# The last task of a two-layer spectral kernel: rows loaded in three narrow transfers, held groups through three pairs of banks, three groups added by GpSimd

## The chip, the cores and the metric

The kernel runs on one core of one Trainium2 chip. The time is device microseconds of one execution; three runs of the kernel before took 517.57 us in the median (516.96 to 521.88). All arithmetic is float32.

## The reference

Input x is (4, 45, 90, 384): batch, height H = 45, width W = 90, channels. Two spectral layers follow each other, and the second starts from the first one's spectrum. In each, a 2-D real FFT over H and W goes to 23 kept columns of W, eight channel blocks of 48 pass through two small matrices with ReLU and softshrink, and an inverse FFT is added to the layer's input:

```python
xf = rfft2(x, axes=(1, 2), norm='ortho')              # 23 columns of W
o1 = relu(blocks(xf) @ w1 + b1)
z  = softshrink(o1 @ w2 + b2, 0.01)                   # second layer: complex
y  = irfft2(z, s=(H, W), axes=(1, 2), norm='ortho') + x
```

## The kernel before, in words

The work is cut into 8 tasks: 4 images times 2 halves of 192 channels. A task's image half lies in one of three SBUF tiles `img` as 90 partitions (w) by 45 x 192.

1. **fwd**: 12 groups of four rows of H (the last has one) are multiplied by the forward matrix of W, and go by way of `fs` (task 0: `f0`) to the scratch `scr_f` in HBM.
2. **Steps**: 23 columns of W make 6 steps of 4 columns a task, 48 steps in all, numbered s = 0 to 47. A step loads its columns into `bt`, and runs the products a, c0, d0, c1, d1, t and e (FFT over H, both layers' matrices, transposes, inverse FFT over H). The result of e is copied by ACT and DVE from bank pair P0 to `et`, and stored by SP to the scratch `scr_i` (L341). Task 7 is steps 42 to 47.
3. **rows** and **inv**: when the six steps of a task are stored, its 46 (48 with padding) rows, a real and an imaginary one for each column, are loaded back (L364) in 5 sets of groups of H, each set as two transfers of 48 partitions (even and odd pairs of rows of H, at partitions 0 and 64), into the three tiles `jr`. For each of 12 groups TensorE multiplies by the inverse matrix of W (L657; two matmuls, each seen as two records), and DVE adds the result to `img` (L587). Then y is stored: by GpSimd's queue for tasks 0 to 6, two groups at a time (L416), by SP's queue group by group for task 7 (L368).

`schedule()` writes one order of kinds by hand, and each engine and each DMA queue walks it in that order, doing its own part; semaphores hold it back. In the steady state the groups of inv of an earlier task stand between the products of a step. At the end no step is left to stand between:

- Task 6's groups g0 to g6 stand in steps 46, 47 and the drain; g7 to g11 ("held") come after e of step 47. All use bank pair P3 (banks 6 and 7), and L639 to L641 make TensorE wait for the add of the group before.
- Then `rows` of task 7: SP waits for the stores of steps 46 and 47 (L347), for each set also until the bank `jr` is free (L356, after a held group's product), for sets 3 and 4 in `bt` until the last a.
- Task 7's groups rotate through four bank pairs (P0 to P3). Groups 1, 4, 7 and 10 (`LAST_POOL`) are copied by ACT from PSUM to `p1` (L492) and added from there by GpSimd (L424); ACT waits for GpSimd's add before it overwrites `p1` (L491). The other eight are added by DVE.

`f0` is used by task 0 alone. TensorE's pair P2 is last used by d1, P1 by c0, d0 and t.

Of the kernel before, what the change touches and what calls it, by code (L numbers as in the profile page):

```python
# [25 lines left out]
GROUPS = -(-H // 4)  # L26
XCH = 8
# [4 lines left out]
LAST_POOL = (1, 4, 7, 10)  # L32
# [74 lines left out]
def schedule():  # L107
# [45 lines left out]
    order += [("rows", TASKS - 1, j) for j in range(len(JSETS))]  # L153
# [4 lines left out]
def spectral_layers(nc, x, wts, const, out, where):  # L158
    ctx = ExitStack()
    with ctx:  # L160
# [63 lines left out]
        j_tail = [sem(f"last_set{j}_loaded") for j in range(JR, len(JSETS))]  # L224
# [20 lines left out]
        def set_rows(t, j):  # L245

            if t == TASKS - 1 and j >= JR:
                return bt[j - JR][:, 0:(JSETS[j][1] - JSETS[j][0]) * 2 * HC].rearrange("p (g c) -> p g c", c=2 * HC)
            return jr[bank_of(t, j)[0]]
# [47 lines left out]
        def _(sp):  # L297
            sp.dma_start(cst[:, :], const).then_inc(c_ld, 16)
            for kind, *what in order:
# [36 lines left out]
                if kind == "e":  # L336
                    s, = what
                    t, i = divmod(s, STEPS)
                    sp.wait_ge(e_act, s + 1)
                    sp.wait_ge(e_dve, s + 1)  # L340
                    sp.dma_start(scr_i[t][STEP * i:STEP * i + STEP].rearrange("k e h c -> (e h) k c"),  # L341
                                 et[s % 2][0:2 * H, :, :]).then_inc(e_st[s % 2], 16)
                if kind == "rows" or (kind == "inv" and what[0] < TASKS - 1 and what[1] in (2, 5)):
                    t, j = what if kind == "rows" else (what[0], jset[what[1]] + JR)
                    k, used = bank_of(t, j)
                    landed = j_tail[j - JR] if t == TASKS - 1 and j >= JR else j_ld[k]
# [5 lines left out]
                    if t == TASKS - 1 and j >= JR:  # L352
                        sp.wait_ge(a_mm, 2 * NT)
                    elif used:
# [4 lines left out]
                    if g0 == GROUPS - 1:  # L359
                        sp.dma_start(set_rows(t, j)[0:2 * KWP, 0, 0:HC], rows[:, 4 * g0, :]).then_inc(landed, 16)  # L360
                    else:
                        four = rows[:, 4 * g0:4 * g1, :].rearrange("q (g r s) c -> q g r (s c)", r=2, s=2)
                        for r in range(2):
                            sp.dma_start(set_rows(t, j)[64 * r:64 * r + 2 * KWP, 0:g1 - g0, :], four[:, :, r, :]).then_inc(landed, 16)  # L364
                if kind == "inv" and what[0] == TASKS - 1:
# [3 lines left out]
            sp.wait_ge(y_last, 16 * GROUPS)  # L369

        @block.gpsimd
        def _(pool):
# [21 lines left out]
            for kind, *what in order:  # L394
# [24 lines left out]
                if kind == "inv" and what[0] == TASKS - 1 and what[1] in LAST_POOL:  # L419
# [4 lines left out]
                    nc.gpsimd.tensor_tensor(y, p1[0:W], y, ALU.add).then_inc(i_pool, 1)  # L424
# [7 lines left out]
        def _(act):  # L432
# [4 lines left out]
            for kind, *what in order:  # L437
# [41 lines left out]
                if kind == "e":  # L479
# [4 lines left out]
                    nc.scalar.activation(et[s % 2][0:2 * H, 0::2, :], ps[0:2 * H, P0, 0:2 * HC].rearrange("p (k c) -> p k c", c=HC), ACT.Copy).then_inc(e_act, 1)  # L484
                if kind == "inv" and what[0] == TASKS - 1 and what[1] in LAST_POOL:
                    t, g = what
                    n, B0 = LAST_POOL.index(g), 2 * (g % 4)
                    act.wait_ge(i_mm, t * GROUPS + g + 1)
                    act.wait_ge(d1_ss, 2 * NT)
                    if n > 0:  # L490
                        act.wait_ge(i_pool, n)  # L491
                    nc.scalar.activation(p1[0:W], ps[0:W, B0:B0 + 2, 0:2 * HC], ACT.Copy).then_inc(i_act, 1)  # L492

        @block.vector
        def _(dve):
# [4 lines left out]
            for kind, *what in order:  # L500
# [76 lines left out]
                if kind == "inv" and (what[0] < TASKS - 1 or what[1] not in LAST_POOL):  # L577
                    t, g = what
                    h0, h1 = hrows(g)
                    B0 = P3 if t < TASKS - 1 else 2 * (g % 4)  # L580
# [9 lines left out]
        def _(pe):  # L590
# [15 lines left out]
            for kind, *what in order:  # L606
# [21 lines left out]
                if kind == "inv":  # L628
                    t, g = what
                    j = jset[g]  # L630
                    k, _ = bank_of(t, j)
                    if g == JSETS[j][0]:
                        if t == TASKS - 1 and j >= JR:
                            pe.wait_ge(j_tail[j - JR], 16 * set_dmas(j))
                        else:
                            pe.wait_ge(j_ld[k], rows_landed(t, j))
                    at = g - JSETS[j][0]
                    if t < TASKS - 1:
                        B0 = P3  # L639
                        vacate(0)  # L640
                        vacate(1)  # L641
                    else:
                        B0 = 2 * (g % 4)
                        if g < 4:
                            pe.wait_ge(i_add, t * GROUPS)
# [128 lines left out]
```

## Time and profile before

| | |
|---|---|
| median of 3 runs | 517.57 us (516.96 to 521.88) |
| the profiled execution | 518.28 us |
| its span in the profile | 516.5 us |
| TensorE matmul busy | 482.8 us, 93% |
| DVE, ACT, GpSimd busy | 307.6, 208.8, 172.4 us |
| DMA | 105.25 MB, 204 GB/s over the span |
| share of the chain that ended last: TensorE, DMA, DVE, GpSimd | 72%, 9%, 7%, 3% |

The profile is one execution taken by the hardware's profiler. Busy time is a share of the whole span; the granted clock is that which TensorE's clock gate let through. The profiled execution's span leaves out 1.8 us around it. "PE" is TensorE's matmul, "PEld" its weight load, POOL is GpSimd, and a "q" behind an engine is its queue of instructions or DMAs.

### The profile page before, as it was taken

How to read it: one execution, taken by the hardware profiler on the slowest of the kernel's cores; microseconds unless marked ns; L12 is line 12 of the kernel's file. 1: busy time of each engine (PE TensorE's matmuls, PEld its weight loads, DVE VectorE, ACT ScalarE, POOL GpSimd, SP SyncE). 2: the span in 40 equal slices, each digit the busy share in tenths (PEclk: the TensorE clock that was granted, in tenths of full speed). 3: DMA queues.
4: the chain of work that ended last, by engine and by line, in shares of the span. 5: the costliest groups of instructions: out<-in, count | busy, mean ns of one | idle time of the engine just before them, and what ended most of it. 6: DMA issues, size and time to landing. Idle time of an engine off the chain costs nothing.

```text
span 516.5 us, 14950 instructions
## 1 busy us (share of the span) xinstructions
PE 482.8 (93%) x6192; PEld 341.7 (66%) x6192; DVE 307.6 (60%) x674; ACT 208.8 (40%) x473; POOL 172.4 (33%) x194
## 2 busy tenths in 40 slices
PE   4979999999999999999999999999999999998773
PEld 1347777676776777767777777767777677876521
DVE  6634465457745676447754677466764577566643
ACT  0025544543444434643355443554354433534201
POOL 9823222223341343213441144213351123222124
PEclk9999999999999999999999999999999999999967
DMA  9999763868889688886899678876889665634397
GB/s 211 262 253 279 203 178 95 179 178 207 251 212 230 171 229 252 193 218 182 256 231 227 177 202 260 233 206 184 267 211 248 165 173 163 146 92 134 110 256 227
DMA packets 77256, 105.25 MB, mean 204 GB/s; under 512 B 7584, under 2 KB 63666, under 8 KB 77190
## 3 DMA queue, kind: packets, MB, share of 16 engines
q1 hardware_dynamic: 57606, 56.74, 41.6%
q0 software_dynamic: 10608, 40.66, 29.5%
q10 hardware_dynamic: 8976, 6.90, 5.7%
q8 instruction: 50, 0.82, 0.7%
q14 instruction: 16, 0.13, 0.1%
HBM read 52.84 MB, written 51.43 MB: 202 GB/s over the span
## 4 chain that ended last, share of the span: by engine, by line
PE 72%; DMA 9%; DVE 7%; POOL 3%; SPq 3%; issue 3%; ACT 2%; POOLq 0%; ACTq 0%
PE ps L657 14%; PE ps L725 12%; PE ps L750 11%; PE ps L712 10%; PE ps L622 9%; PE ps L670 7%; PE ps L737 4%; DMA scr_i<-et 4%; DMA scr_f<-fs 4%; PE ps L688 4%; PE ps L698 2%; DVE img L587 2%; SPq L364 2%; POOL xs L407 2%; DVE ns L561 2%
## 5 line engine op out<-in xcount | busy, mean ns | idle before, releaser
L587 DVE TENSOR_TENSOR img<-ps,img 90x768 f32<-90x768 f32 x92 | 82.6, 900 | 21.7 <-PE ps L657 18.1
L407 POOL TENSOR_TENSOR xs<-xs,nt 128x360 f32<-128x360 f32 (+1 forms) x48 | 41.5, 865 | 146.3 <-DVE nt L539 120.5
L657 PE MATMUL ps<-jr,cst 64*90 64x384 f32 (+1 forms) x358 | 81.7, 526 | 7.7 <-DVE img L587 5.4
L416 POOL DMA_DIRECT2D y<-img x42 | 34.7, 826 | 133.8 <-DVE img L587 133.4
L622 PE MATMUL ps<-img,cst 128*64 128x384 f32 (+1 forms) x368 | 72.5, 510 | 7.2 <-DMA img<-x 6.4
L471 ACT ACTIVATE o<-ps,wt 97x180 f32<-97x180 f32 (+1 forms) x96 | 33.8, 406 | 104.6 <-PE ps L712 104.6
L561 DVE SCALAR_TENSOR_TENSOR ns<-p,ps 109x384 f32<-109x384 f32 x96 | 53.1, 553 | 37.7 <-ACT p L478 32.8
L725 PE MATMUL ps<-wt,o 128*64 128x96 f32 x1472 | 73.9, 249 | 0.1
L725 PEld LDWEIGHTS ps<-wt,o 128*64 128x64 f32 x1472 | 64.9, 137 | 12.3 <-issue 12.3
L712 PE MATMUL ps<-xs,wt 64*97 64x180 f32 (+1 forms) x768 | 68.0, 313 | 3.9 <-POOL xs L407 3.5
L750 PE MATMUL ps<-ns,cst 64*90 64x192 f32 x736 | 71.0, 322 | 0.0
L670 PEld LDWEIGHTS ps<-cst,bt 128*64 128x64 f32 x1472 | 61.0, 137 | 14.9 <-issue 13.7
L750 PEld LDWEIGHTS ps<-ns,cst 64*90 64x90 f32 x736 | 62.8, 155 | 8.3 <-issue 1.6
L670 PE MATMUL ps<-cst,bt 128*64 128x90 f32 x1472 | 66.6, 243 | 0.5 <-DMA bt<-scr_f 0.5
L712 PEld LDWEIGHTS ps<-xs,wt 64*97 64x97 f32 x768 | 56.7, 158 | 15.7 <-POOL xs L407 9.7
L478 ACT ACTIVATE p<-ps 109x384 f32<-109x384 f32 x96 | 47.0, 490 | 27.3 <-PE ps L725 27.3
L445 ACT ACTIVATE fs<-ps 112x384 f32<-112x384 f32 x84 | 38.9, 475 | 38.9 <-PE ps L622 26.3
L553 DVE TENSOR_SCALAR o<-ps,wt 97x180 f32<-97x180 f32 (+1 forms) x96 | 33.8, 394 | 33.5 <-PE ps L712 33.5
L569 DVE TENSOR_TENSOR ns<-ps,ns 109x192 f32<-109x192 f32 x96 | 29.8, 352 | 33.5 <-PE ps L737 32.7
L515 DVE COPY xs<-ps 128x360 f32<-128x360 f32 (+1 forms) x48 | 24.8, 517 | 39.9 <-PE ps L670 39.9
L622 PEld LDWEIGHTS ps<-img,cst 128*64 128x64 f32 x368 | 24.9, 142 | 35.6 <-issue 31.5
L400 POOL TENSOR_TENSOR xd<-xs 128x360 f32<-128x360 f32 (+1 forms) x48 | 38.0, 792 | 27.6 <-DVE xs L515 27.6
(43 smaller groups left out, 413.6 us busy)
## 6 DMA issues: line engine op xcount, KB each, us to landing
y<-img POOLq DMA_DIRECT2D x35, 540.0 KB, 5.7
img<-x POOLq DMA_DIRECT2D x25, 540.0 KB, 8.5
scr_i<-et SPq DMA_DIRECT2D x48, 270.0 KB, 5.8
scr_f<-fs SPq DMA_DIRECT2D x154, 72.0 KB, 3.2
bt<-scr_f SPq DMA_DIRECT2D x40, 270.0 KB, 5.0
jr<-scr_i SPq DMA_DIRECT2D x48, 216.0 KB, 5.2
img<-x ACTq DMA_DIRECT2D x10, 576.0 KB, 8.5
y<-img SPq DMA_DIRECT2D x11, 270.0 KB, 3.3
```

Of the source, the lines that this page charges most:

```text
L400: nc.gpsimd.tensor_tensor(xd[:, :, 0:kws(s) * H].rearrange("p q (k m) -> p q k m", m=H), xt[:, :, :, 0:H], xt[:, :, :, H:2 * H], ALU.subtr ...
L407: nc.gpsimd.tensor_tensor(re, re, nt[s % 2][:, :, 0:kws(s), 0:H], ALU.subtract).then_inc(re_ok, 1)
L445: nc.scalar.activation(fs[k][0:rows, 0:cols], ps[0:rows, P3 + g % 2, 0:cols], ACT.Copy).then_inc(f_cp, 1)
L478: nc.scalar.activation(p1[0:rows, p, :], ps[0:rows, P2 + p, 0:2 * HC], ACT.Relu).then_inc(d1_p, 1)
L561: nc.vector.scalar_tensor_tensor(out=ns[0:rows, p].rearrange("p n r c -> p (n r c)"), in0=p1[0:rows, p, :], scalar=2 * LAM, in1=ps[0:rows, ...
L587: nc.vector.tensor_tensor(y, p, y, ALU.add).then_inc(i_add, 1)
L622: last = mm(ps[64 * r:64 * r + 64, P3 + g % 2, 0:(b - a) * HC], K["w_fwd"], img[t % IMGS][:, a:b, :].rearrange("p h c -> p (h c)"), start= ...
L657: last = mm(ps[0:W, B0 + r, 0:n], K["w_inv"][64 * r:64 * r + 64, :], set_rows(t, j)[64 * r:64 * r + 64, at, 0:n], start=True, stop=True)
L670: last = mm(ps[64 * ab:64 * ab + 64, P0 + q, k * 2 * H:(k + 1) * 2 * H], bt[s % BT][:, at:at + 64], K["h_fwd"], start=True, stop=True)
L712: last = mm(ps[0:2 * BS + 1, P2 + ab, q * STEP * H:q * STEP * H + n], w1[k, im, 2 * f + q, :], xt[k, q, 0:kws(s), im * H:(im + 1) * H], st ...
L725: last = mm(ps[64 * r:64 * r + 64, P2 + p, b * 2 * BS:(b + 1) * 2 * BS], o11[:, b, 2 * p + r, :], w21[:, block_no(s // STEPS, b), :], star ...
L750: last = mm(ps[0:2 * H, P0 + r, p * HC:(p + 1) * HC], K[("h_inv_re", "h_inv_im")[im]][k, :], ns[k, p, :, im, :], start=im == 0, stop=im == 1)
```

## The change

Three things, all for the end of the program:

- **Rows of task 7 in three transfers.** `f0`, free since task 0, takes all 12 groups. After the store of step 44 is issued, SP waits for the stores of steps 42 and 43 and loads the 16 rows (8 columns, real and imaginary) that they hold, for all groups: two DMAs of 16 partitions x 11 x 384 and one for the last group's single row. The same after the store of step 46 for steps 44 and 45. The last 16 rows are loaded after the stores of 46 and 47, one half and the single row on SP's queue, the other half on ACT's. TensorE waits once, before g0. The products contract 48 rows instead of 64.
- **Held groups through three pairs.** g7 takes P2, g8 P1, g9 P3, g10 P2, g11 P1. g7 waits for the last reader of d1's banks, g8 for those of d0's and t's, g9 as before for the add of the group before it, g10 and g11 for the add of the group three before. Task 7's g1 to g3 wait for the last held user of their pair.
- **GpSimd adds three groups.** `LAST_POOL` is (1, 4, 7); ACT copies by turns to `p1` and to `et[0]`. The stores of these three groups are issued by ACT, after its last copy, and SP stores the other nine.

```diff
+HELD = 7
-LAST_POOL = (1, 4, 7, 10)
+LAST_POOL = (1, 4, 7)
...
+        def last_rows(m, r):
+            k0, k1 = 4 * STEP * m, 4 * STEP * (m + 1)
+            rows = scr_i[TASKS - 1].rearrange("k e h c -> (k e) h c")[k0:k1]
+            four = rows[:, 0:H - 1, :].rearrange("q (g r s) c -> q g r (s c)", r=2, s=2)[:, :, r, :]
+            return four, f0[64 * r + k0:64 * r + k1, 0:GROUPS - 1, :], rows[:, H - 1, :], f0[k0:k1, GROUPS - 1, 0:HC]
+        def held_no(t, g):
+            return g - HELD if t == TASKS - 2 else -1
+        def pair_of(t, g):
+            if t == TASKS - 1:
+                return (P0, P1, P2, P3)[g % 4]
+            return (P2, P1, P3)[held_no(t, g) % 3] if held_no(t, g) >= 0 else P3
...
 SP, after the store of a step
+                    if t == TASKS - 1 and i in (2, 4):
+                        for n in (s - 2, s - 1):
+                            sp.wait_ge(e_st[n % 2], 16 * (n // 2 + 1))
+                        for r in range(2):
+                            four, to, one, to_one = last_rows(i // 2 - 1, r)
+                            sp.dma_start(to, four).then_inc(l_ld[0], 16)
+                        sp.dma_start(to_one, one).then_inc(l_ld[0], 16)
...
+                if kind == "last_rows":
+                    for n in (NT - 2, NT - 1):
+                        sp.wait_ge(e_st[n % 2], 16 * (n // 2 + 1))
+                    four, to, one, to_one = last_rows(STEPS // 2 - 1, 0)
+                    sp.dma_start(to, four).then_inc(l_ld[0], 16)
+                    sp.dma_start(to_one, one).then_inc(l_ld[0], 16)
...
 ACT
+                    if n > 1:
+                        act.wait_ge(i_pool, n - 1)
+                    p = (p1[0:W], et[NT % 2][0:W].rearrange("p (r s) c -> p r (s c)", r=2))[n % 2]
+                    nc.scalar.activation(p, ps[0:W, B0:B0 + 2, 0:2 * HC], ACT.Copy).then_inc(i_act, 1)
+            for n, g in enumerate(LAST_POOL):
+                h0, h1 = hrows(g)
+                act.wait_ge(i_pool, n + 1)
+                act.dma_start(out[b, h0:h1, :, f * HC:(f + 1) * HC].rearrange("h w c -> w h c"), img[(TASKS - 1) % IMGS][0:W, h0:h1, :]).then_inc(y_last_act, 16)
...
 TensorE, tasks before the last
+                        if n == 0:
+                            pe.wait_ge(d1_ss, 2 * NT)
+                        elif n == 1:
+                            pe.wait_ge(d0_ss, 2 * NT)
+                            pe.wait_ge(t_add, 2 * NT)
+                        elif n >= 3:
+                            pe.wait_ge(i_add, t * GROUPS + g - 2)
+                        else:
+                            vacate(0)
+                            vacate(1)
```

On TensorE, at the held groups and the first groups of the last task, the order before (the names in brackets are the semaphores waited for; inv_added counts DVE's adds):

```order
L750 MATMUL ps<-ns,cst 90x192 x5
L657 MATMUL ps<-jr2,cst 90x384 [waits inv_added]
L657 MATMUL ps<-jr0,cst 90x384 [waits inv_added,j0_loaded]
L657 MATMUL ps<-jr1,cst 90x192 [waits inv_added,j1_loaded]
L657 MATMUL ps<-jr2,cst 90x384 [waits d0_shrunk,e_copied_act,t_added,e_copied_dve,inv_added,j2_loaded]
```

and now:

```order
L793 MATMUL ps<-ns,cst 90x192 x5
L700 MATMUL ps<-jr2,cst 90x384 [waits d1_shrunk]
L700 MATMUL ps<-jr2,cst 90x384 [waits t_added,d0_shrunk]
L700 MATMUL ps<-jr0,cst 90x384 [waits inv_added,j0_loaded]
L700 MATMUL ps<-jr0,cst 90x384 [waits inv_added]
L700 MATMUL ps<-jr1,cst 90x192 [waits inv_added,j1_loaded]
L700 MATMUL ps<-f0,cst 90x384 [waits e_copied_act,e_copied_dve,last_rows1_loaded,last_rows0_loaded]
```

No product has moved; g7 and g8 no longer wait for an add, and the last task's rows are waited for once, at its first group.

On SP's queue, from the store of step 44 to the first store of the last y, the order before:

```order
L341 DMA scr_i7<-et0 90x4x192 [waits e_copied_dve,e_copied_act]
L364 DMA jr0<-scr_i6 48x2x384 [waits inv_product]
L341 DMA scr_i7<-et1 90x4x192 [waits e_copied_dve,e_copied_act]
L360 DMA jr1<-scr_i6 48x192 [waits inv_product]
L364 DMA jr2<-scr_i7 48x3x384 [waits inv_product,e0_stored,e1_stored]
L364 DMA jr0<-scr_i7 48x3x384 [waits inv_product]
L364 DMA bt0<-scr_i7 48x2x384 [waits a_product]
L360 DMA bt1<-scr_i7 48x192 [waits a_product]
L368 DMA y<-img1 90x4x192 [waits inv_added]
```

and now:

```order
L354 DMA scr_i7<-et0 90x4x192 [waits e_copied_dve,e_copied_act]
L361 DMA f0<-scr_i7 16x11x384 [waits e1_stored,e0_stored]
L362 DMA f0<-scr_i7 16x192
L381 DMA jr0<-scr_i6 48x2x384 [waits inv_product]
L354 DMA scr_i7<-et1 90x4x192 [waits e_copied_dve,e_copied_act]
L377 DMA jr1<-scr_i6 48x192 [waits inv_product]
L386 DMA f0<-scr_i7 16x11x384 [waits e1_stored,e0_stored]
L387 DMA f0<-scr_i7 16x192
L391 DMA y<-img1 90x4x192 [waits inv_added] x8
```

The loads of scr_i7 for the first and second thirds now stand directly behind the stores of steps 44 and 46, ahead of the last row sets of task 6; of the nine transfers behind the last step's store two are left here, and one more stands on ACT's queue.

## Rows read from the trace of the kernel before

**Rows 1.** The page, part 2: tenths in 40 slices of the span, TensorE's clock and DMA.

```profile
PEclk9999999999999999999999999999999999999967
DMA  9999763868889688886899678876889665634397
```

**Rows 2.** Chain that ended last, in order of time: start us, us, what.

```profile
462.34 0.65 PE ps L657 x4
...
488.13 0.96 DVE img L587
...
489.23 0.90 PE ps L657 x4
...
492.17 0.96 DVE img L587
...
493.27 1.60 PE ps L657 x4
...
497.40 6.46 PE ps L657 x20
...
510.37 1.80 POOL img L424
```

**Rows 3.** Windows, L657 alone: us, PE busy (x), PEld busy (x), PEclk, DMA share, GB/s.

```profile
492.00:494.00 2.00, 0.86 (x5) 0.41 (x4) 0.77 0.90 239
...
502.00:504.00 2.00, 2.00 (x11) 0.88 (x9) 0.67 0.87 304
...
506.00:508.00 2.00, 2.00 (x14) 0.80 (x10) 1.00 0.71 201
...
510.00:512.00 2.00, 0.00 (x0) 0.00 (x0) 0.54 0.93 266
```

**Rows 4.** Groups by form, 486 to 517: shapes xcount | busy us, mean ns | idle before.

```profile
L587 DVE TENSOR_TENSOR img<-ps,img 90x768 f32<-90x768 f32 x12 | 11.3, 952 | 8.8 <-PE ps L657 8.7
L424 POOL TENSOR_TENSOR img<-p,img 90x768 f32<-90x768 f32 x4 | 7.2, 1800 | 6.6 <-ACT p L492 6.6
L492 ACT ACTIVATE p<-ps 90x768 f32<-90x768 f32 x4 | 3.2, 806 | 19.1 <-PE ps L657 15.1 <-POOL img L424 4.0
```

**Rows 5.** DMA queues in 491-493, 493-495, 495-497, 501-503, 509-514: packets, MB, share.

```profile
q0 software_dynamic: 103, 0.43, 92.8%
q1 hardware_dynamic: 12, 0.02, 3.1%
...
q1 hardware_dynamic: 279, 0.40, 71.7%
...
q0 software_dynamic: 117, 0.48, 87.3%
q1 hardware_dynamic: 45, 0.05, 13.6%
...
q1 hardware_dynamic: 328, 0.34, 56.7%
q0 software_dynamic: 89, 0.32, 46.2%
...
q1 hardware_dynamic: 1813, 1.34, 92.0%
```

**Rows 6.** Lines L364 (490 to 491.2) and L368: xcount, issue ns, starts; landing.

```profile
L364 SPq DMA_DIRECT2D jr<-scr_i x2: 308/860/1411, 490.7 to 491.0; - x2
...
DMA to landing us min/median/max: 4.6/4.9/5.3
...
L368 SPq DMA_DIRECT2D y<-img x12: 329/495/988, 500.5 to 512.9; - x12
...
DMA to landing us min/median/max: 2.6/3.3/4.2
```

**Rows 7.** Timelines of POOL and DVE: start us, us, what, idle before and releaser.

```profile
493.53 0.81 POOL L416 DMA_DIRECT2D y<-img  x1 [3.18 <-DVE img L587]
...
496.95 0.35 DVE L587 TENSOR_TENSOR img<-ps,img 90x192 f32<-90x192 f32 x1 [1.10 <-PE ps L657]
```

More of the change, by code:

```diff
@@ L152, in schedule @@
     order += held
-    order += [("rows", TASKS - 1, j) for j in range(len(JSETS))]
+    order.append(("last_rows",))
     order += [("inv", TASKS - 1, g) for g in range(GROUPS)]
@@ L223, in spectral_layers @@
         j_ld = [sem(f"j{k}_loaded") for k in range(JR)]
-        j_tail = [sem(f"last_set{j}_loaded") for j in range(JR, len(JSETS))]
+        l_ld = [sem(f"last_rows{k}_loaded") for k in range(2)]
+        y_last_act = sem("y_of_last_task_stored_act")
         i_mm, i_add = sem("inv_product"), sem("inv_added")
@@ L359, in _ @@
                     if g0 == GROUPS - 1:
-                        sp.dma_start(set_rows(t, j)[0:2 * KWP, 0, 0:HC], rows[:, 4 * g0, :]).then_inc(landed, 16)
+                        sp.dma_start(jr[k][0:2 * KWP, 0, 0:HC], rows[:, 4 * g0, :]).then_inc(j_ld[k], 16)
                     else:
@@ L363, in _ @@
                         for r in range(2):
-                            sp.dma_start(set_rows(t, j)[64 * r:64 * r + 2 * KWP, 0:g1 - g0, :], four[:, :, r, :]).then_inc(landed, 16)
-                if kind == "inv" and what[0] == TASKS - 1:
+                            sp.dma_start(jr[k][64 * r:64 * r + 2 * KWP, 0:g1 - g0, :], four[:, :, r, :]).then_inc(j_ld[k], 16)
+                if kind == "last_rows":
[4 more added lines that the diff above has]
+                    sp.dma_start(to_one, one).then_inc(l_ld[0], 16)
+                if kind == "inv" and what[0] == TASKS - 1 and what[1] not in LAST_POOL:
                     g, (h0, h1), (b, f) = what[1], hrows(what[1]), divmod(TASKS - 1, HALVES)
@@ L423, in _ @@
                     y = img[t % IMGS][0:W, h0:h1, :].rearrange("p (r s) c -> p r (s c)", r=2)
[L424 removed]
+                    p = (p1[0:W], et[NT % 2][0:W].rearrange("p (r s) c -> p r (s c)", r=2))[n % 2]
+                    nc.gpsimd.tensor_tensor(y, p, y, ALU.add).then_inc(i_pool, 1)
                 if kind == "load" and what[0] % STEPS == 3 and what[0] // STEPS >= 2:
@@ L629, in _ @@
                     t, g = what
[L630 to L645, printed above, removed]
-                            pe.wait_ge(t_add, 2 * NT)
-                            pe.wait_ge(d0_ss, 2 * NT)
+                    B0, n = pair_of(t, g), held_no(t, g)
+                    if t == TASKS - 1:
+                        if g == 0:
+                            pe.wait_ge(l_ld[0], 16 * (3 * (STEPS // 2 - 1) + 2))
+                            pe.wait_ge(l_ld[1], 16)
                             pe.wait_ge(e_act, NT)
                             pe.wait_ge(e_dve, NT)
+                        elif g < 4:
+                            users = [m for m in range(HELD, GROUPS) if pair_of(TASKS - 2, m) == B0]
+                            pe.wait_ge(i_add, (TASKS - 2) * GROUPS + (users[-1] if users else HELD - 1) + 1)
                         elif g - 4 in LAST_POOL:
@@ L656, in _ @@
                         n = min(2, h1 - h0 - 2 * r) * HC
-                        last = mm(ps[0:W, B0 + r, 0:n], K["w_inv"][64 * r:64 * r + 64, :], set_rows(t, j)[64 * r:64 * r + 64, at, 0:n], start=True, stop=True)
+                        last = mm(ps[0:W, B0 + r, 0:n], K["w_inv"][64 * r:64 * r + live, :], rows[64 * r:64 * r + live, 0:n], start=True, stop=True)
                     last.then_inc(i_mm, 1)
```

33 lines of the change are left out of this document (19 added, 14 removed).

## The prediction

> **What bounds the kernel now.** I read the page's slices first. TensorE's row of granted clock is at full speed until the last two of 40 slices, and there the DMA row stands at 9 and 7 [rows 1]. So only the last 26 us differ from the steady state, and they are also all that the change rewrites for compute; what it moves earlier is DMA work. Next comes the chain of waits, in order of time [rows 2]. It shows how the end is built. From 488.1 on the held groups of task 6 take turns: one group's product (0.90), its add (0.96), then the next product, because all use bank pair P3; the last of these adds ends at 497.3 [rows 7]. At 493.27 a product takes 1.60 instead of 0.90. From 497.40 the products of the last task run, five groups in 6.46 us, 1.29 each, where a group at full clock takes 0.65 (462.34). The chain ends in GpSimd's add at 510.37, after which come two stores and the end at 516.5.
>
> The windows of 2 us say why products are slow [rows 3]: the granted clock falls inside 492 to 494 (mean 0.77), with TensorE busy 0.86 of each 2 us, and is back at 1.00 after 502 to 504 (mean 0.67, so at about 503.3), 5.9 us after work became continuous. The two levels are 1.2 and 2.4 GHz. The same rows give the DMA share: in the eleven windows from 492 to 514 it is never under 0.71 (506 to 508) and mostly around 0.9. That is the second bound. In 509 to 514 only stores of y run, at 1.34 MB in 5 us [rows 5], so one store of 276 KB costs 1.03 us of all engines. A store lands 2.6 us after its issue at the least [rows 6], and the last is issued at 512.9. Durations: an add of DVE 0.95, ACT's copy 0.81, GpSimd's add 1.80 [rows 4].
>
> **The change, part by part.**
>
> *Held groups through three pairs.* Removed: the turn-taking. New: g7 into P2 and g8 into P1 wait for nothing late, so g8's product follows g7's at once and its add follows g7's add (which ends at 489.1 [rows 2]): end at 490.1 instead of 491.1. g9 falls into the branch that waits for the last add issued before it, which is g8's, although P3 was free since g6; so one turn of the old kind remains: product from 490.2, 0.90, add until 492.1. g10 and g11 then run add after add, and the last held add ends at 493.4 instead of 497.3. That is 3.9 us, but it is gained before the last task's rows have landed, so it is worth nothing by itself. What is late next is those rows. It has a side effect: GpSimd's stores of g8, g9 and of g10, g11, now issued at 493.53 and 497.61, are issued about 1.1 and 3.8 us earlier, since a store follows its add by 0.4 us (493.13 to 493.53 [rows 2, 7]).
>
> *Rows in three transfers of 16 partitions.* Each moves 2 x 16 x 11 x 1536 B + 16 x 768 B = 0.553 MB. The first two leave at the stores of steps 44 and 46, where SP's queue has nothing pressing: behind the second stands only the 36 KB row set of g11, needed at 491.7. I cost them at nothing; the cover is the product chain of the steps, which reads none of this. Six issues on SP of 0.3 to 1.4 us each [rows 6] would be the price without it, and a late store of step 47. So 1.1 MB leaves the tail. The waits on banks and bt go too.
>
> The third goes out from SP and ACT when the store of step 47 has landed; today's first rows wait for the same store and are issued at 490.7 [rows 6]. When does it land? The trace has no transfer of 16 partitions; the nearest is that pair of 48 partitions. Beside GpSimd's store (q0; SP's queue is q1), already streaming, that pair moves 0.02 MB in 491 to 493, then 0.40 MB in 493 to 495 [rows 5], and its second half lands at 491.0 + 5.3 = 496.3 [rows 6]. I use the same rates. 0.02 MB by 493; then 0.20 MB per us until the next GpSimd store arrives. That store is issued at about 492.5, and its bytes come 1.4 us after the issue (today 493.53, and in 495 to 497 it holds the engines [rows 5, 7]), so at 493.9: 0.18 MB more. 0.35 MB is left. Beside a GpSimd store a transfer that has just begun gets 0.05 MB in 2 us (495 to 497), one that is under way 0.34 MB in 2 us (501 to 503) [rows 5]. The rows will be under way, so I take 0.17 MB per us: 2.1 us, to 496.0. By these rates today's pair of 0.44 MB would be through at 495.1 and landed 1.2 us later with a store in its last part; I add 1.0. **The rows land at R = 497.0.** Bounds: no sharing at all, 493.0 + 0.533 / 0.20 + 1.0 = 496.7; starved at 0.025 until both GpSimd stores (0.9 MB at 0.24) are through at 497.6, then 0.20, gives 499.9. Today's first product of the last task starts at 497.4, so the start hardly moves: what the held groups gained is spent waiting for the third transfer.
>
> *The last twelve groups.* TensorE idles from 492 to R, and today the clock fell with more work than that, and again in 510 to 512 (mean 0.54), with no product left [rows 3]. So g0 to g3 run at 1.29 each, the first released after 1.60, and I let the clock rise at R + 5, a little before today's 5.9, because today's stretch holds a wait of 1 us. Adds of DVE end at R + 2.6 (g0), 5.1 (g2), 6.4 (g3), 7.7 (g5), 8.7 (g6), 9.7, 10.6, 11.6, 12.0. Stores land 2.6 us after that or 1.03 after the one before: R + 5.2, 7.7, 9.0, 10.3, 11.3. The three GpSimd groups no longer take turns on p1: g1 is added at R + 5.6, g4 at 8.9, g7 at 10.8. But their stores stand on ACT's queue behind its last copy (g7's, which ends at R + 9.0), so g1's store leaves 3.4 us after its add. From there DMA is the bound: six whole stores (g1, g4, g8, g9, g7, g10) at 1.03 after R + 11.3, then a quarter store, 0.6, and 0.3 from the last landing to the end as today. The end is R + 18.4 with these roundings, that is 515.4.
>
> *GpSimd adds three groups, not four.* DVE takes g10 (0.95) and GpSimd's last add moves from 512.2 to about 507.8. Today this is the chain's end, and I would count 4 us, but the stores behind it already land one after another, 1.03 apart, so most of it stays. It is in the sum above.
>
> Sum: 515.4 against 516.5, 1.1 us less. The profiled execution took 518.28, 0.7 above the median of 517.57, so the forecast for the median is 517.57 - 1.1 = **516.5 us**. Around 1% (5 us) can be told from no change.
>
> **Rivals.**
> 1. *The third transfer is slow because it is narrow* (slower). Its halves touch 16 partitions each. For it: no row shows such a transfer, and all fast loads here use 48 partitions or more. Against: sixteen partitions of eleven pieces give all 16 engines work, and the pieces are the same 1536 B. It decides where the rows stream at less than 0.13 MB per us: then R passes 498.1 and the kernel is slower. At a third of today's 0.20, as a third of the partitions would have it, R is 493.0 + 8.0 + 1.0 = 502.0 and the median 521.5. The Trainium skill, "SBUF — State Buffer", section "Door 1: The DMA port swizzle", says that 16 partitions reach 4 of 16 ports, 104 GB/s measured at 1 MiB, and that two transfers to different halves gain only 6%; my estimate from that page is 0.553 MB in about 5 us, R near 498.9 and a median of 518.4. No run here shows it yet. Chance of this rival, with the starved bound of 499.9 (median 519.4): 0.20.
> 2. *The clock stays up, or the stores are fed without gaps.* TensorE's idle stretch before R is the shorter the earlier the rows land. At full clock g0's store lands at R + 4.5, ten more follow at 1.03, and the end is R + 15.7 = 512.7, median 513.8. For it: the clock fell only after 5 us of half-busy work. Against: 5 us of idleness before R. Chance 0.14.
> 3. *The bytes were the bound, and moving 1.1 MB out of the tail is worth its full time*, 1.1 / 0.27 = 4.1 us: 513.5, and with the 2.7 us of rival 2 on top 510.8. For it: DMA share 0.90 and more over 20 us [rows 3]. Against: the third transfer and the y stores of task 6 must pass before any y of task 7 exists. Chance 0.06.
> 4. *An early transfer gets in the way*: the second, 0.55 MB beside GpSimd's store of g4 and g5, could hold back the store of step 47, and everything behind it, by up to its own 2 us; and more if the steps feel it. Chance 0.05, nearly all of it still within 1%, but 0.03 beyond with rival 1.
>
> **How the numbers follow.** Forecast 0.55: R between 496.7 and 498.1 gives 516.2 to 517.6. Rival 1 reaches to 519.4 and, with little chance, 521.5; rival 2 down to 513.8, or 513.4 with R at its early bound. Leaving out rival 3, rival 1's far end and rival 4's, the range is 513.4 to 519.3. Faster by over 1% (below 512.4) is rival 3: 0.06. Slower by over 1% (above 522.7) needs rivals 1 and 4 together: 0.04. Within 1%: 0.90.
>
> **What the new profile would show.** Right: the last held add ends near 493.4, then TensorE idles until about 497 with the idle time put down to DMA f0<-scr_i; the clock row is at 0.50 when g0 starts; the last five stores land about 1.03 apart with the DMA share at 0.9; ACT's three stores are issued after its last copy. Wrong: first product of the last task before 496 or after 498.5; a clock of 1.00 throughout; stores that land with gaps at the end, which would make DVE's adds the bound; any lengthening before 488.

## The result, and the profile after

The changed kernel takes 519.3 us (median of 20 runs, 516.45 to 522.22), the kernel before 517.5 us in the same comparison (20 runs, 514.58 to 521.88): ratio 1.0037, interval 1.0021 to 1.0053. It is 1.8 us slower, and the forecast was 1.1 us faster. Two more comparisons of the same kernel, on two chips, gave 1.0043 and 1.0025 (again and again2, below). All ratios are of executions in the chip's faster state; one execution of pool_only took 782.35 us at a granted clock of 0.56 and is left out of its ratio. The profiled execution took 520.9 us, its span is 519.1.

The page's second part of the changed kernel, TensorE's granted clock and the DMA share in 40 slices:

```profile
PEclk9999999999999999999999999999999999999967
DMA  9999763858888698887899679977889664737667
```

The clock row reads as before [rows 1]. The chain of waits in order of time (start, us, what) shows what has changed behind it:

```profile
489.25 2.99 DMA scr_i<-et
...
492.67 6.46 DMA f<-scr_i
499.13 0.04 issue
499.18 9.53 PE ps L700 x36
508.71 0.02 issue
508.73 1.82 DVE img L624 x2
...
511.42 0.26 DVE img L624
```

The held groups have left the chain, and so has GpSimd's add at its end [rows 2]. In their place stands a wait for a transfer (6.46), and behind it TensorE runs nine of the twelve groups' products without a pause. The windows of 2 us, all engines, say at what speed (columns: us, PE, PEld, DVE, ACT, POOL busy, granted clock, DMA share, GB/s):

```profile
496.00:498.00 2.00, 0.00 (x0) 0.00 (x0) 0.00 (x0) 0.00 (x0) 0.00 (x0) 0.50 1.07 225
...
500.00:502.00 2.00, 2.00 (x10) 0.92 (x8) 0.95 (x1) 0.00 (x0) 0.00 (x0) 0.50 0.04 14
502.00:504.00 2.00, 2.00 (x10) 0.92 (x8) 0.63 (x1) 0.81 (x1) 1.02 (x1) 0.50 0.50 138
504.00:506.00 2.00, 2.00 (x8) 0.87 (x8) 1.28 (x2) 0.07 (x1) 0.78 (x1) 0.50 0.35 91
506.00:508.00 2.00, 2.00 (x14) 0.92 (x12) 1.20 (x2) 0.74 (x1) 1.18 (x1) 0.95 0.64 186
508.00:510.00 2.00, 2.00 (x16) 0.98 (x12) 1.88 (x3) 0.81 (x1) 1.66 (x2) 1.00 0.62 158
510.00:512.00 2.00, 0.29 (x2) 0.00 (x0) 1.68 (x3) 0.00 (x0) 0.78 (x1) 1.00 0.95 267
```

The DMA engines, in the old kernel never under 0.71 from 492 to 514 [rows 3], now stand at 0.04 in 500 to 502 and at 0.35 to 0.64 until 510. TensorE is fully busy then, at half its clock (0.50, that is 1.2 GHz) until about 506. The bytes that used to load rows are gone from the tail, and nothing has come up to use the room: the y that could be stored is still being computed. The timelines of TensorE and ACT (start, us, what; idle before, releaser) show one more thing:

```profile
499.18 11.12 PE L700 MATMUL ps<-f,cst 48*90 48x384 f32 x46 [6.05 <-DMA f<-scr_i]
```

```profile
502.09 0.81 ACT L523 ACTIVATE p<-ps 90x768 f32<-90x768 f32 x1 [12.87 <-PE ps L700]
505.93 0.81 ACT L523 ACTIVATE et<-ps 90x768 f32<-90x768 f32 x1 [3.03 <-PE ps L700]
508.09 0.81 ACT L523 ACTIVATE p<-ps 90x768 f32<-90x768 f32 x1 [1.35 <-PE ps L700]
508.10 3.05 ACTq L528 DMA_DIRECT2D y<-img  x3
```

TensorE waits 6.05 us for the rows. GpSimd's add of group 1, released by the copy at 502.09, ends at 504.78, but ACT's first store leaves at 508.10, when its last copy has begun: 3.3 us in which that store, 1.03 us of DMA work, could have run beside a share of 0.35.

### The profile page after: what moved, and what is told of

It is laid out like the page before. It is cut to its first block, busy times and chain, and to the rows that moved or that the text cites. A ratio compares the mean times of both kernels' runs of the same rounds, so it can differ in the third digit from the quotient of the medians.

```text
span 519.1 us, 14940 instructions
## 1 busy us (share of the span) xinstructions
PE 479.4 (92%) x6192; PEld 342.1 (66%) x6192; DVE 307.7 (59%) x675; ACT 208.2 (40%) x472; POOL 170.6 (33%) x193
## 4 chain that ended last, share of the span: by engine, by line
PE 75%; DMA 8%; DVE 5%; POOL 3%; issue 2%; ACT 2%; ACTq 1%; SPq 1%; DVEq 0%; POOLq 0%
PE ps L700 13%; PE ps L768 13%; PE ps L793 12%; PE ps L755 11%; PE ps L659 9%; PE ps L713 7%; PE ps L780 4%; PE ps L731 4%; PE ps L741 3%; DMA img<-x 2%; DMA scr_i<-et 2%; DMA scr_f<-fs 2%; POOL xs L430 2%; DVE ns L598 2%; ACT p L502 1%
## 5 line engine op out<-in xcount | busy, mean ns | idle before, releaser
L624 DVE TENSOR_TENSOR img<-ps,img 90x768 f32<-90x768 f32 (+1 forms) x93 | 83.2, 901 | 22.3 <-PE ps L700 18.6
L659 PE MATMUL ps<-img,cst 128*64 128x384 f32 (+1 forms) x368 | 70.8, 498 | 9.4 <-DMA img<-x 9.2
L700 PE MATMUL ps<-jr,cst 64*90 64x384 f32 (+1 forms) x322 | 70.9, 502 | 3.8 <-DVE img L624 2.0
```

The source lines that it names most:

```text
L624: nc.vector.tensor_tensor(y, p, y, ALU.add).then_inc(i_add, 1)
L659: last = mm(ps[64 * r:64 * r + 64, P3 + g % 2, 0:(b - a) * HC], K["w_fwd"], img[t % IMGS][:, a:b, :].rearrange("p h c -> p (h c)"), start= ...
L700: last = mm(ps[0:W, B0 + r, 0:n], K["w_inv"][64 * r:64 * r + live, :], rows[64 * r:64 * r + live, 0:n], start=True, stop=True)
```

## How the runs are compared

The issue of step 47's store, S here, lies at 488.04 in the old kernel's profile and at 489.25 in the new one's, but over all profiles of this study, whose programs differ little before it, it lies anywhere from 484.14 to 489.40. So a span says nothing about the tail. From the issue of step 43's store to S, on the other hand, it is 31.03 to 31.05 us in nineteen of the twenty profiles (31.33 in warm): the early transfers do not slow the steps, and what they cost lies behind S. The table therefore counts from S, in us: landing of the last rows that the first product waits for, end of the last task's first add, end of the span. Each row is one profiled execution; the ratio is that of the timed runs (10 to 20 each) to the kernel before on the same chip. The same program, the change, ends 29.84, 29.11 and 28.59 us after S in its three profiles, so tails that differ by less than about 1.3 us in one profile each are not told apart.

| kernel | ratio (95%) | rows | first add | end |
|---|---|---|---|---|
| before | | 8.26 | 11.94 | 28.43 |
| the change | 1.0037 (1.0021 to 1.0053) | 9.88 | 12.51 | 29.84 |
| again | 1.0043 (1.0022 to 1.0064) | 10.18 | 12.81 | 29.11 |
| again2 | 1.0025 (1.0005 to 1.0045) | 10.03 | 12.66 | 28.59 |
| undo_rows | 1.0006 (0.9975 to 1.0036) | 8.43 | 11.06 | 29.87 |
| undo_held | 0.9998 (0.9972 to 1.0024) | 9.66 | 12.29 | 28.48 |
| undo_pool | 1.0006 (0.9986 to 1.0026) | 10.37 | 13.00 | 28.48 |
| rows_only | 1.0021 (1.0003 to 1.0040) | 10.01 | 12.64 | 28.76 |
| held_only | 1.0010 (0.9984 to 1.0036) | 8.59 | 11.22 | 28.34 |
| pool_only | 0.9990 (0.9970 to 1.0010) | 8.14 | 11.24 | 28.20 |
| warm | 1.0026 (1.0001 to 1.0051) | 9.67 | 14.86 | 29.75 |
| warm8 | 0.9969 (0.9947 to 0.9991) | 9.84 | 11.77 | 26.15 |
| warm_rows | 1.0013 (0.9980 to 1.0046) | 8.30 | 10.23 | 30.04 |
| before_warm | 0.9981 (0.9966 to 0.9995) | 8.03 | 12.01 | 27.45 |
| act_early | 1.0004 (0.9982 to 1.0025) | 9.82 | 12.45 | 28.17 |
| best | 0.9983 (0.9962 to 1.0003) | 9.96 | 11.89 | 25.99 |
| late_y | 1.0032 (1.0010 to 1.0054) | 10.07 | 12.70 | 29.09 |
| late_all | 1.0038 (1.0014 to 1.0062) | 8.72 | 11.35 | 29.94 |
| no_second | 1.0023 (1.0000 to 1.0046) | 10.42 | 13.05 | 29.16 |
| wide | one execution, 517.7 us | 9.43 | 12.06 | 28.09 |

## Experiments: which part costs it

**again, again2**: the change, unedited, beside the experiments of its chip.

> The changed kernel once more, unedited, for a second profile and for times on the chip of the three runs beside it. If the length of the half-clock stretch is fixed by the program, it lasts again about 10.2 us and ends 7.0 us after the first product of the last task; if it depends on where the execution meets the clock's control, it ends at another distance, and the end of the span moves with it by 1 to 3 us.

> The changed kernel as it is, for its difference to before on the chip of the three runs with one part each: 1.5 to 2.2 us slower than before by every theory (0.3 to 0.4 per cent).

Measured 519.02 and 518.34 us. The loss is real and is 0.25 to 0.43%; sizes under some 0.2% can't be told apart here. The half-clock stretch lasted 6.8 us in both instead of 10.2, so the program does not fix its length, and the end came earlier with it.

**undo_rows, undo_held, undo_pool**: the change with one part taken back. The held groups' edit is the shortest:

```diff
-            return g - HELD if t == TASKS - 2 else -1
+            return -1
...
-            return (P2, P1, P3)[held_no(t, g) % 3] if held_no(t, g) >= 0 else P3
+            return P3
... (task 7's g1 to g3 get back the waits for d1, d0 and t)
```

undo_rows puts the five sets of rows back behind step 47's store; undo_pool gives g10 back to GpSimd, with one buffer p1 and all stores of y on SP.

> The changed kernel with the rows of the last task loaded as before (five sets of 48 partitions behind the last step's store); held groups and GpSimd's three groups stay. Theory A (the tail is paced by TensorE's half clock after an idle wait): the first product starts earlier, set by set, but the clock has fallen all the same, so from the first product to the end it stays near the 19.9 us of the changed kernel; total about 517.5, the kernel before's. Theory B (one wait for all rows, which land 6.8 us after their issue, costs what is lost): step 47's store to the first product shrinks from 9.9 to 8.5 us or less, and the kernel is faster than the changed one by 1.5 us or more and at least as fast as before.

> The changed kernel with all held groups through bank pair P3 again. Theory A: the held products last until about 9 us after step 47's store, the clock falls later or not before the rows land, and the last groups reach full clock earlier: faster than the changed kernel by 1 to 2 us. Theory B with GpSimd's stores in the way: GpSimd's stores of task 6 are issued 1 and 3 us later, the rows land about 1 us earlier (5.8 us after their issue): faster by about 1 us. If neither holds: within 0.3 us of the changed kernel's 519.3.

> The changed kernel with GpSimd adding groups 1, 4, 7 and 10 from one buffer and SP storing all groups in order. Theory C (the stores that stand behind ACT's last copy cost the loss): faster than the changed kernel by 1 us or more. Theories A and B: GpSimd's chain of copy and add takes turns again, so the same or slower by up to 1.5 us (519.3 to 521).

Measured 517.75, 517.3 and 517.57 us beside 517.2 for before: whichever part is taken back, no loss is left that can be told from nothing. The intervals reach 1.0036, 1.0024 and 1.0026, and the unedited change was not run on this chip, so that the whole loss is gone is likely and not shown. undo_held and undo_pool came out as theories A and C said, the rows landing 6.3 us after their issue in undo_held, not 5.8. By its time undo_rows meets both of its theories; its one profile speaks against that of one late wait for all rows. Its chain and VectorE's first add of the last task:

```profile
494.00 8.00 DMA jr<-scr_i
501.99 0.04 issue
502.04 5.54 PE ps L696 x24
```

```profile
498.14 0.95 DVE L615 TENSOR_TENSOR img<-ps,img 90x768 f32<-90x768 f32 x1 [5.05 <-PE ps L696]
```

The first add ends 1.45 us earlier from S than in the change, the end is the same (29.87): the second set of rows lands only at S + 13.97, and products at half clock do the rest.

**rows_only, held_only, pool_only**: one part kept, the other two taken back.

> Only the three transfers of rows are left of the change: held groups through P3 alone as before, GpSimd adds four groups, all stores on SP. Theory that the parts cost only together (the held part makes TensorE's pause long, the rows part makes all twelve groups wait for one late transfer, the GpSimd part sends the early stores late): 517.5, within 0.2 per cent of before, the rows landed 9.5 to 10.4 us after the issue of step 47's store. Rival, each part has a price of its own: the rows' part alone costs what it cost in the change, 1.5 to 2 us, 519.3. A gain of 1 us or more would say that the rows were worth what the prediction wanted and the other two parts ate it.

> Only the held groups through three pairs are left of the change; the rows come in before's five sets, GpSimd adds four groups, all stores on SP. Theory that the parts cost only together: within 0.2 per cent of before, the last held add about 4 us earlier than in before (near 5 us after the issue of step 47's store instead of 9.3), the first add of the last task a little earlier than before's 11.9 us, the end the same, since half the clock takes back the start. Rival, a price of its own for the longer pause of TensorE: 1 to 2 us slower. Rival, an earlier start is an earlier end: 1 us or more faster.

> Only the GpSimd part is left of the change: three groups on GpSimd, their stores on ACT's queue behind ACT's last copy, g10 on VectorE; rows in before's five sets, held groups through P3. Theory that the parts cost only together: within 0.2 per cent of before; what it gains at the end (no GpSimd add behind the last product) it loses by sending the store of group 1 late. Rival, the deferred store has a price of its own: 1 to 2 us slower, 518.5 to 519.5. Rival, the chain's end was GpSimd's last add: 1 us or more faster.

Measured 518.11, 518.02 and 516.69 us, beside 517.32 for before. Only the rows' interval lies above 1; on this chip the three transfers alone (1.0021) cost nearly what the whole change cost (again2, 1.0025). That lies between the two expectations (within 0.2%, or 519.3) and decides neither. The other parts alone can't be told from nothing: the held part's 4 us of earlier work (its last add at S + 5.06 instead of 9.3) shows no gain by itself, as forecast.

## Experiments: half the clock while the DMA engines idle

**warm, warm8**: products on a constant into free banks keep TensorE busy during the wait for the rows.

```diff
                         if g == 0:
+                            pe.wait_ge(e_act, NT)
+                            pe.wait_ge(e_dve, NT)
+                            for n in range(8):      # warm: 14
+                                mm(ps[0:64, P0 + n % 2, 0:2 * HC], K["w_fwd"], cst[:, 0:2 * HC], start=True, stop=True)
                             pe.wait_ge(l_ld[0], 16 * (3 * (STEPS // 2 - 1) + 2))
```

> The changed kernel with 14 products of constants, whose results are overwritten, on TensorE between the last held group and the first group of the last task, to keep its clock up while the rows land (some 4.5 us of work at full clock, in a wait of 6 us). Theory A: the granted clock is 1.00 when the first group starts, and from there to the end it takes 16 to 17 us instead of 19.9: 515.5 to 516.5 in the median. Theory B: the rows set the start and the stores the end, so the clock gives at most 1 us: 518.3 or more.

> The changed kernel with 8 products of constants in the wait for the rows. With 14 of them each took 0.66 us, so they ran 3.4 us past the landing of the rows; 8 take 5.3 us and end half a us before it. Theory A (the half clock makes the products late, and the engines that move data stand half idle until the products come): the clock is 1.00 from the first product on, first product about 9.8 us after step 47's store is issued, end about 26.5 us after it instead of 29.8: 515.5 to 516.5 in the median, faster than the changed kernel by 3 us and than the kernel before by 1 to 2. Theory D (the end is set by the bytes of the last stores whatever the clock): 518.5 to 519.5.

The timeline of TensorE in warm:

```profile
491.01 9.24 PE L673 MATMUL ps<-cst 128*64 128x384 f32 x28
500.18 7.65 PE L704 MATMUL ps<-f,cst 48*90 48x384 f32 x46
```

and in warm8:

```profile
493.11 5.37 PE L673 MATMUL ps<-cst 128*64 128x384 f32 x16
499.18 7.65 PE L704 MATMUL ps<-f,cst 48*90 48x384 f32 x46 [0.70 <-DMA f<-scr_i]
```

In both, the last task's products take 7.65 us instead of 11.12. In warm each filler took 0.66 us, twice what the expectation reckoned; together they ran 3.4 us beyond the rows' landing (S + 13.0 against 9.67), and the gain went there: 518.99 us. With eight of them a short wait is left (0.70). The windows of warm8 (its S is within 0.05 us of the change's) show the clock at 1.00, and the DMA share at 0.80 and more from 502 on, where in the change it is 0.35 to 0.64 until 510:

```profile
500.00:502.00 2.00, 2.00 (x16) 1.03 (x14) 1.55 (x2) 0.81 (x1) 0.35 (x1) 1.00 0.07 24
502.00:504.00 2.00, 2.00 (x15) 0.97 (x12) 1.88 (x3) 0.81 (x1) 1.88 (x2) 1.00 0.80 218
504.00:506.00 2.00, 2.00 (x14) 0.97 (x12) 1.88 (x3) 0.81 (x1) 1.88 (x2) 1.00 0.86 243
```

515.59 us: 3.4 us less than again on the same chip, and less than before. So the half clock costs the change's tail some 3.4 us. It is not the only thing that does: act_early, below, gains with the clock at half.

**before_warm, warm_rows**: two fillers behind each of the held groups g7 to g11 of the kernel before; and undo_rows with six fillers ahead of g0.

> The kernel before with 2 products of constants behind each held group (1.3 us of the 1.35 us that TensorE waits for the add). Theory A holds for the kernel before too: the clock stays at 1.00 from step 47 to the end; the end moves little, since its DMA share is 0.87 or more from 492 on: 27.5 to 28.4 us after step 47's store (28.4 now), 516.0 to 517.0. If the clock was worth as much there as in the changed kernel: 25 to 26, 514 to 515.

> The kernel with the rows as before (five sets behind the last step's store), held groups and GpSimd's three groups as changed, and 6 products of constants ahead of the last task's first group. It tells what the early rows are worth when the clock is up. If the bytes in the tail count (1.1 MB, 4 us of all DMA engines): end 28 us or more after step 47's store, against 26.2. If only the clock counted: 26.5 or less.

TensorE in before_warm (us, busy, granted clock, DMA share, GB/s):

```profile
494.00:500.00 6.00, 5.39 (x22) 1.00 0.94 222
```

before_warm gains 0.19%, about 1 us (516.57), so the kernel before paid for the clock too, but less. In warm_rows the first add came at S + 10.23; then TensorE waited 3.43 us for the second set of rows, and the clock was at half from S + 13.9 to 17.3: 518.96, no gain to be seen. With all rows in place before the first product, as in warm8, it is at 1.00 until the products are done.

## Experiments: the rows' landing, and ACT's stores

**late_y, late_all**: GpSimd's stores of groups 8 to 11 of task 6 wait for the rows' landing; in late_all those of 6 and 7 too.

```diff
+                    if t == TASKS - 2 and g == 9:       # late_all: g == 7
+                        pool.wait_ge(l_ld[0], 16 * (3 * (STEPS // 2 - 1) + 2))
+                        pool.wait_ge(l_ld[1], 16)
                     pool.dma_start(out[b, r0:r1, ...
```

> The changed kernel with GpSimd's last two stores of task 6 (groups 8 to 11, 0.9 MB) held back until the last rows have landed. If GpSimd's stores starve the rows: the rows land 5.3 us after their issue instead of 6.8, and the first product comes 1.5 us earlier; the end moves by as much under theory A if the clock rises as much earlier, else by less than 0.5. If the narrow transfer is slow by itself: they land 6.5 us or more after their issue as now, and the end is the same or later, since 0.9 MB is moved behind.

> All three of GpSimd's stores that stand near the third transfer (groups 6 and 7, 8 and 9, 10 and 11 of task 6) wait until it has landed, so the last rows have the DMA engines to themselves from their issue on. Theory that the narrow transfer itself sets the landing: still 6.0 us or more from issue to landing, as with two of the three stores out of the way (6.4), and the time within 1 us of the change. Rival, the running store of groups 6 and 7 takes the rows' turn for some 2 us: landing 4.0 to 5.0 us after the issue, near 8 us after the issue of step 47's store, first add 1.5 to 2 us earlier; the end moves less, since the clock is at half and 0.9 MB of stores now stand ahead of the last task's first ones: 517.5 to 519.

late_y: 518.51 us, landing 6.4 us after the issue instead of 6.7 to 6.8; the two later stores are not what holds the rows. late_all, the half on ACT's queue, the queues between 492.5 and 494.5 (packets, MB, share; q1 is SP's, q10 ACT's), and the chain:

```profile
L516 ACTq DMA_DIRECT2D f<-scr_i x1: 350/350/350, 491.0 to 491.0; - x1
...
DMA to landing us min/median/max: 5.1/5.1/5.1
```

```profile
q10 hardware_dynamic: 158, 0.24, 58.8%
q1 hardware_dynamic: 148, 0.20, 45.6%
```

```profile
491.33 4.95 DMA f<-scr_i
496.28 0.04 issue
496.32 9.00 PE ps L703 x36
```

With the DMA engines to themselves the rows take 5.3 us, between the two expectations (4.0 to 5.0, or 6.0 and more): the three stores cost them 1.4 to 1.5 us, of which the running one of groups 6 and 7 about 1.1 (5.3 against late_y's 6.4). And they move 0.43 MB in 2 us, 0.22 MB per us, so transfers of 16 partitions are no slower here than the 0.20 that the prediction took from the pair of 48 [rows 5]. They land at S + 8.72, before the forecast's 8.96, and the kernel is as slow as the change (519.31): the products still take 9.00 at a fallen clock, and the stores that were put off stand in the way of the last task's, whose first one lands 6.9 us after its issue instead of 2.6.

**wide**: the third transfer as 48 partitions of four groups, nearly the same bytes (0.59 MB). It leaves out the last third of the rows of groups 4 to 10.

> The changed kernel with its third transfer taken over 48 partitions and groups 0 to 3 instead of 16 partitions and groups 0 to 10: 0.59 MB instead of 0.55, in pieces of the same 1536 B, issued at the same moment. It leaves out the last third of the rows of groups 4 to 10. If the transfer is slow because it is narrow: it lands 5.3 us after its issue, as the pair of 48 partitions did before, instead of 6.6. If the wait is for its turn behind GpSimd's store: 6.5 or more, as now.

The rows land 6.4 us after the first issue, not 5.3. The twelve profiles with the narrow transfer beside the same store show 6.3 to 7.7, so this one execution shows no gain from the width.

**no_second**: the second early transfer is left out.

```diff
-                    if t == TASKS - 1 and i in (2, 4):
+                    if t == TASKS - 1 and i == 2:
... (TensorE's wait for the rows is lowered by the three DMAs left out)
```

> Leaves out the second of the two early transfers (the rows of steps 44 and 45), so the last task's products read old rows there; the third transfer and all else are the change's. Theory that this transfer, still in the queues, is what makes step 47's store land 3.0 to 3.3 us after its issue in the kernels with it, where those without it show 2.6: the store lands at 2.6 to 2.7, the rows at 9.3 instead of 9.9 to 10.2, and the median is 0.5 to 0.7 us under that of the change. Rival, GpSimd's store issued at 484.5 holds it back by itself: landing still at 3.0 or later, time unchanged.

The issue of step 47's store and its landing, in the change and in no_second:

```profile
L354 SPq DMA_DIRECT2D scr_i<-et x1: 335/335/335, 489.3 to 489.3; - x1
...
DMA to landing us min/median/max: 3.0/3.0/3.0
```

```profile
L354 SPq DMA_DIRECT2D scr_i<-et x1: 318/318/318, 487.5 to 487.5; - x1
...
DMA to landing us min/median/max: 2.6/2.6/2.6
```

The store lands at 2.63, as in the six other profiles without that transfer (2.62 to 2.64); the thirteen with it show 2.99 to 3.62. GpSimd's store of groups 4 and 5, issued 4.75 us before S, goes the same way: with the second early transfer it lands 2.2 to 2.8 us after S, without it 0.5 us before it. But the rows, issued 0.36 us earlier, landed at 10.42, no earlier than in the change, and the ratio (1.0023) is among the change's own. The first half of the expectation held, the second did not: in the one profile the late store of step 47 does not set the landing.

**act_early, best**: ACT's stores of y among its copies (that of g1 behind the second copy, those of g4 and g7 behind the third), instead of all behind the last copy, so only g1's moves; best joins that with warm8.

```diff
+                    for n in (() if n == 0 else (0,) if n == 1 else (1, 2)):
+                        h0, h1 = hrows(LAST_POOL[n])
+                        act.wait_ge(i_pool, n + 1)
+                        act.dma_start(out[b, h0:h1, ...
... (the same loop behind the last copy is taken out)
```

> The changed kernel with ACT's store of group 1 issued right after its copy of group 4, ahead of its copy of group 7. The store leaves about 1.3 us earlier, into a stretch where the DMA share is 0.64. Theory C (the stores behind ACT's last copy cost the loss): faster by about 1 us, 518.3. Theory A: the products feed the stores too slowly for one store's place to matter more than 0.5 us: 518.8 to 519.3.

> The changed kernel with 8 products of constants in the wait and ACT's store of group 1 ahead of its last copy. With 8 products alone the DMA engines are full from about 17 us after step 47's store on; one store earlier fills the gap before that: end 25.5 to 26.2 us after step 47's store (26.2 with the 8 products alone), 514.5 to 515.6 in the median, faster than the kernel before by 0.3 to 0.5%.

ACT's timeline in act_early:

```profile
500.65 0.81 ACT L523 ACTIVATE et<-ps 90x768 f32<-90x768 f32 x1 [2.92 <-PE ps L700]
500.65 0.58 ACTq L528 DMA_DIRECT2D y<-img  x1
502.58 0.81 ACT L523 ACTIVATE p<-ps 90x768 f32<-90x768 f32 x1 [1.13 <-PE ps L700]
503.38 2.26 ACTq L528 DMA_DIRECT2D y<-img  x2
```

The first store leaves at S + 16.5, in the change at S + 18.8. 516.89 us: 2.1 us less than again on the same chip (by the spread of the twelve runs each, an estimate of 0.7 to 2.9); theory C had asked for about 1. The clock plays no part in it: its half-clock stretch is 10.2 us long, as in the change's first profile. best took 515.9 us, 0.9983 of before with an interval that reaches 1.0003, and has the shortest tail of the profiles (25.99); that it beats warm8 isn't shown. warm8 (0.9969) and before_warm (0.9981) are shown to be faster than the kernel before, and their intervals overlap; best and before_warm, on one chip, differ by 0.7 us with intervals that overlap too. So with the clock kept up in both kernels, it isn't shown that the change gains anything.

## Why the prediction was wrong

**Two terms of the sum were too short: the landing R of the rows, and the last one, "the last twelve groups: the end is R + 18.4".** The forecast's end, 515.4, is S + 27.4. The change's three profiles end 2.5, 1.8 and 1.2 us later. R takes 0.9, 1.2 and 1.1 us of that, and the last term the rest: the end came at R + 19.96, 18.93 and 18.56. As a step of the argument the last one failed: it makes the end follow R one for one, and counts on the DMA bound to cover ACT's late stores. The runs show that the tail waits for y to store: full clock behind the same R is worth 3.4 us (warm8), one store sent 2.3 us earlier 2.1 us (act_early), and rows that land 1.2 us earlier nothing (late_all).

1. *Held groups.* Right: the last held add ends at S + 5.06 (forecast 493.4, S + 5.4), with no gain to be seen alone (held_only).
2. *R.* Forecast S + 9.0, measured 9.9 to 10.2, beside the break-even that the prediction named (498.1, S + 10.06). The rate was read rightly, its end was not. The forecast has all 0.55 MB through by 496.0, S + 8.0. In the change's profile 0.51 MB are through by 497.2, just as late after S, and then the rows' last 0.04 MB take another 1.1 us, in which GpSimd's store moves 0.30 (497.2 to 498.3; q0 is GpSimd's):

```profile
q0 software_dynamic: 75, 0.30, 83.4%
q10 hardware_dynamic: 24, 0.03, 16.4%
q1 hardware_dynamic: 20, 0.01, 6.9%
```

The landing follows 0.9 us behind the last packet, as forecast (1.0). Taking GpSimd's stores away brings R to S + 8.72 (late_all). Step 47's store does land 0.4 to 0.7 us later because of the second early transfer (the small end of rival 4, shown by no_second), but without that the rows land no earlier. Rival 1's reason, the narrowness, isn't borne out: the transfer runs at 0.22 MB per us when alone, where rival 1 needed less than 0.13.

3. *What R is worth.* Not its own length. late_all's rows came 1.2 us earlier and undo_rows' first add 1.45 us earlier, and neither ended earlier, though both put other transfers into the tail. The end goes with the moment at which stores of y begin to land one behind the other: from the landing of the fourth store (21.25 after S in the change, 18.72 in warm8, 20.12 in act_early) it is 7.4 to 8.6 us to the end in these three, and 7.1 to 9.1 in all twenty, whose ends lie between 26.0 and 30.0. That is a pattern of the profiles and no test.
4. *The clock.* "Rises at R + 5": measured R + 7.1, 5.6 and 4.8, with ends at R + 19.96, 18.93 and 18.56. So where the clock rose as forecast the last term is right within 0.2 us, and its miss goes with the clock's delay. Rival 2 was priced nearly rightly (2.7 us forecast, 3.4 measured with warm8). A shorter wait did not bring it about: after 1.86 us of waiting in undo_held and 4.89 in late_all the clock was at half all the same; work in the wait did.

```profile
497.22 9.98 PE L703 MATMUL ps<-f,cst 48*90 48x384 f32 x46 [1.86 <-DMA f<-scr_i]
```

5. *ACT's stores.* The 3.4 us of delay were read rightly (3.3) and then costed at nothing, with the DMA bound as cover. The prediction's own landings, five in the 6.1 us from R + 5.2 to R + 11.3, left room for another store there. In the change's first profile only four had landed by R + 11.4. act_early puts a price of about 2 us on it.
6. *GpSimd adds three.* Its add left the chain's end as forecast, and the last stores do land under a DMA share of 0.94 to 0.95. Alone, the part is not told from nothing (0.9990).

The lower end of the prediction's range comes out at 513.5 by its own terms, not 513.4; nothing hangs on it.

What stays open: why the change is slower than the kernel before, and not only no faster, and how the loss is shared among the parts. The rows alone cost 0.2%, but the two pairs that hold the rows show no loss (undo_held, undo_pool), and the three together cost 0.25 to 0.43%; such sizes are near what the timing resolves. That undo_held is saved by a shorter pause of TensorE ahead of the rows (1.86 us idle before the first product instead of 6.05) fits its profile and isn't shown.

## What to carry to other kernels

Bytes taken out of a tail are worth only what the next limit can use: ask at what rate the results come that would be stored in the room, and at which clock the engine makes them. A wait that an engine spends idle near the end can be filled with work sized to end at the landing; here fourteen fillers, which overran it, lost what eight gained. A store issued from an engine that also copies stands behind its copies in program order, so its place among them is part of the schedule. And try a remedy on the kernel before as well: fillers helped both kernels here.

## What the hardware showed beyond that

- A stretch at half clock was 10.2 us long in the change's profile (S + 6.7 to 16.9) and 6.8 us in again and again2, the same kernel.
- The rows landed 9.7 to 10.4 us after S in the twelve profiles whose third transfer has 16 partitions and GpSimd's store of groups 6 and 7 beside it, though they were issued anywhere from S + 2.7 to 3.7; with that store moved away too (late_all) they landed at 8.7.
- Two transfers of 16 partitions each, from the queues of SP and ACT and alone on the DMA engines, moved 0.43 MB in 2 us (late_all), no less than the 0.40 MB that two of 48 partitions from SP alone moved from 493 to 495 beside the end of a store of GpSimd's [rows 5].
